# Graph attention on one core: probabilities turned in 32x32 squares on VectorE and moved by DMA instead of turned on TensorE, and the next keys and queries placed between the last slots

## The chip, the core and the metric

One core of a Trainium2 chip runs the whole program. The metric is the device time of one execution in microseconds, lower is better. The engines have their own instruction queues and meet at semaphores: TensorE (PE, matrix products into PSUM), VectorE (DVE), ScalarE (ACT), GpSimd (POOL), and SyncE (SP), which here only issues DMAs.

## The reference

Eight batches of x (1024 x 384, fp32) pass through masked attention with six heads of 64, an output projection, a residual and a layer norm:

```python
q = _heads(seq_inputs @ Wq + bq)
k = _heads(seq_inputs @ Wk + bk)
v = _heads(seq_inputs @ Wv + bv)
scores = jnp.einsum('bhqd,bhkd->bhqk', q, k) / np.sqrt(HEAD_SIZE)
bias = jnp.where(graph_mask, 0.0, NEG)[:, None]
probs = jax.nn.softmax(scores + bias, axis=-1)
ctx = jnp.einsum('bhqk,bhkd->bhqd', probs, v)
...
x = _layernorm(x + (ctx @ Wf + bf), axis=-1)
```

## The kernel before, in words

**Pieces.** Projections and scores are products of fp32r halves: each operand is split into a high part and a low part, and three products (high-high, high-low, low-high) are summed (three_products, L354 to L356). The probabilities times v are plain fp32, which the profile shows as two matmuls for each one written.

**Slots.** A batch is 24 slots. A slot takes 128 queries and the two heads of one pair. Its two units (one head each) go through this chain:

- PE: scores (L444, 12 matmuls) into score_ps, which holds one slot; the next slot's scores wait until both units are masked.
- DVE: one pass adds the mask and takes the row minimum (mask_scores, L660), from PSUM into prob.
- ACT: the exponential with row sums (exponential, L559).
- PE: turn (L457): eight 128x128 transposes of a unit, four into each half of turn_ps.
- ACT and DVE copy the halves into prob_t, keys on the partitions (copy_first L568, copy_odd_second L574, copy_even_second L669).

Two slots (256 queries, one pair) make a pair of slots that is mixed with v: mix (L470), 32 matmuls in two chunks, into context_ps. DVE divides by the row sums (divide, L683). For this the inverse sums must lie along the free axis on every partition: DVE inverts and transposes them (L674, L677), SP writes them to DRAM in four DMAs (L305) and reads them back in two broadcasts (L310). ACT and POOL split the context into high and low (L582, L806).

**Jobs.** Between the slots' chains PE does the jobs of the batch: v (eight), q for the later queries, x transposes of the next batch (L362), output projections p (eight), each with its place in the tables MID, MID_NEXT, AHEAD and TAIL. A k, q or x job is taken out by one ACT pass (high part, L548, L553) and one DVE pass (low part, L645, L650); v by DVE with its bias (L636); p by DVE, which adds the residual and takes moments (L689, L696, L701). The next batch's six k jobs and three first q jobs stand after slot 23, in TAIL. The normalisation is Newton steps and scaling on POOL (L823 to L827, L265). POOL also makes the masks (L788) and adds the output bias to the residual (L802). SP loads x and adjacency and stores the output at fixed slots.

**Order.** The order of each engine is written out by hand in its body(), and an engine works through its queue in order.

## Time and profile before

| | |
|---|---|
| runs | 1510.48 us median of 3 (1510.31 to 1511.2) |
| the profiled execution | 1509.4 us, its span 1507.4 us |
| TensorE busy | 1471.1 us, 98% |
| VectorE busy | 898.2 us, 60% |
| ScalarE busy | 873.4 us, 58% |
| GpSimd busy | 378.2 us, 25% |
| mean granted TensorE clock | 0.997 of full speed |
| the hardware DMA queue | 47,744 packets, 49.12 MB |

All times are of one profiled execution. Busy time is the time in which an engine executes something; matmuls are pipelined, so the price of a group of matmuls is read from the chain of work, where the pieces touch, and not from the duration of one.

### The profile page before, as it was taken

The page shows a single profiled execution, that of the slowest core. Times are in us where ns is not written, and L with a number is a line of the kernel's source. Part 1 is how long each engine was busy: PE and PEld are TensorE (multiplying, and loading weights), DVE is VectorE, ACT ScalarE, POOL GpSimd, SP SyncE. Part 2 cuts the span into 40 slices and gives each one's busy share as a digit, 9 for nine tenths or more (in the row PEclk, how much of TensorE's full clock was granted, in tenths as well). Part 3 has the DMA queues.
Part 4 walks back from the last instruction along what each step waited for, and adds up shares of the span by engine and source line. Part 5 has one row for each costly group of instructions (what it writes and reads, how often), then busy time and mean ns, then how long its engine had stood idle before and what let it go on. Part 6 is the DMA issues. An engine that isn't in the chain of part 4 may idle for free.

```text
span 1507.4 us, 32054 instructions
## 1 busy us (share of the span) xinstructions
PE 1471.1 (98%) x11088; PEld 1141.7 (76%) x11088; DVE 898.2 (60%) x1769; ACT 873.4 (58%) x1637; POOL 378.2 (25%) x676
## 2 busy tenths in 40 slices
PE   7999999999999999999999999999999999999996
PEld 6777787777877778777787777877778777787764
DVE  5666645665556655666555665566655666465654
ACT  4566626666266662666636665366654666546662
POOL 2112242122411224122141221412214122141222
PEclk9999999999999999999999999999999999999998
DMA  3110101100011000100001100011001110000000
GB/s 129 36 40 30 29 27 38 38 29 29 27 50 29 29 29 24 50 30 29 30 24 50 40 29 20 29 49 35 29 19 37 50 29 30 15 25 19 30 22 28
DMA packets 47925, 51.41 MB, mean 34 GB/s; under 512 B 9089, under 2 KB 47745, under 8 KB 47745
## 3 DMA queue, kind: packets, MB, share of 16 engines
q1 hardware_dynamic: 47744, 49.12, 10.5%
q8 instruction: 100, 1.64, 0.5%
q14 instruction: 81, 0.66, 0.1%
HBM read 36.31 MB, written 12.78 MB: 33 GB/s over the span
## 4 chain that ended last, share of the span: by engine, by line
PE 92%; DVE 3%; issue 2%; ACT 1%; POOL 1%; DMA 0%; DVEq 0%; SPq 0%; ACTq 0%; POOLq 0%
PE turn_ps L457 23%; PE context_ps L470 22%; PE score_ps L444 20%; PE misc_ps L356 4%; PE misc_ps L355 4%; PE misc_ps L354 4%; PE score_ps L354 3%; PE score_ps L355 3%; PE score_ps L356 3%; DVE prob L660 1%; PE context_ps L354 1%; PE turn_ps L354 1%; PE context_ps L356 1%; PE context_ps L355 1%; PE misc_ps L362 1%
## 5 line engine op out<-in xcount | busy, mean ns | idle before, releaser
L660 DVE CUSTOM_DVE_ANT_0 prob<-score_ps,mask 128x1024 f32<-128x1024 f32 x384 | 455.0, 1222 | 252.5 <-PE score_ps L444 232.7
L568 ACT ACTIVATE prob_t<-turn_ps 128x512 f32<-128x512 f32 x384 | 229.5, 598 | 431.6 <-PE turn_ps L457 431.6
L559 ACT ACTIVATE prob<-prob,row_min 128x1024 f32<-128x1024 f32 x384 | 442.1, 1151 | 64.3 <-DVE row_min L660 64.3
L457 PE MATMUL turn_ps<-ident,prob 128*128 128x128 f32 x3072 | 413.1, 276 | 9.8 <-ACT prob_t L568 5.5
L457 PEld LDWEIGHTS turn_ps<-ident,prob 128*128 128x128 f32 x3072 | 337.7, 140 | 94.8 <-issue 78.0
L470 PE MATMUL context_ps<-prob_t,v_all 128*64 128x256 f32 x3072 | 372.1, 385 | 0.8 <-ACT prob_t L568 0.8
L470 PEld LDWEIGHTS context_ps<-prob_t,v_all 128*64 128x64 f32 x3072 | 204.6, 136 | 148.9 <-issue 64.0
L806 POOL TENSOR_TENSOR context_lo<-context,context_hi 128x256 fp32r<-128x256 f32 x96 | 70.6, 735 | 938.6 <-ACT context_hi L582 938.6
L669 DVE COPY prob_t<-turn_ps 128x512 f32<-128x512 f32 x192 | 131.7, 686 | 30.7 <-PE turn_ps L457 30.2
L444 PE MATMUL score_ps<-k_hi,q_hi 64*128 64x512 f32 x768 | 140.9, 444 | 4.8 <-issue 3.8
L444 PE MATMUL score_ps<-k_lo,q_hi 64*128 64x512 f32 x768 | 120.4, 390 | 0.0
L444 PE MATMUL score_ps<-k_hi,q_lo 64*128 64x512 f32 x768 | 119.6, 388 | 0.0
L574 ACT ACTIVATE prob_t<-turn_ps 128x512 f32<-128x512 f32 x192 | 115.3, 600 | 0.0
L265 POOL TENSOR_SCALAR res<-res,mean_var,inv_dev 128x384 f32<-128x384 f32 x62 | 102.0, 1651 | 6.7 <-POOL inv_dev L827 6.7
L788 POOL TENSOR_SCALAR mask<-adj_in 128x1024 f32<-128x1024 uint8 x64 | 67.2, 1050 | 86.8 <-DVE row_min L660 62.7
L444 PEld LDWEIGHTS score_ps<-k_hi,q_hi 64*128 64x128 f32 x768 | 57.2, 184 | 38.8 <-issue 37.5
L444 PEld LDWEIGHTS score_ps<-k_lo,q_hi 64*128 64x128 f32 x768 | 72.5, 184 | 17.0
L444 PEld LDWEIGHTS score_ps<-k_hi,q_lo 64*128 64x128 f32 x768 | 72.6, 184 | 16.4
L650 DVE SCALAR_TENSOR_TENSOR k_lo<-score_ps,bias_qk,k_hi 128x512 fp32r<-128x512 f32 x48 | 36.0, 750 | 77.5 <-ACT k_hi L553 77.5
L354 PE MATMUL score_ps<-xt_hi,weight_hi 128*128 128x512 f32 (+1 forms) x216 | 78.6, 364 | 0.7 <-DVE k_lo L650 0.7
L553 ACT ACTIVATE k_hi<-score_ps,bias_qk 128x512 fp32r<-128x512 f32 x48 | 33.1, 690 | 76.3 <-PE score_ps L356 74.6
L355 PE MATMUL score_ps<-xt_lo,weight_hi 128*128 128x512 f32 (+1 forms) x216 | 76.7, 355 | 0.0
(85 smaller groups left out, 1834.9 us busy)
## 6 DMA issues: line engine op xcount, KB each, us to landing
x_in<-in_x_dram SPq DMA_DIRECT2D x32, 384.0 KB, 3.4
inv_rows<-spread_dram SPq DMA_DIRECT2D x192, 64.0 KB, 2.6
out_dram<-res SPq DMA_DIRECT2D x32, 384.0 KB, 2.5
adj_in<-in_adj_dram SPq DMA_DIRECT2D x64, 128.0 KB, 2.2
spread_dram<-inv_turned SPq DMA_DIRECT2D x384, 0.5 KB
prob_t<-in_L_gnn_Wk_dram SPq DMA_DIRECT2D x1, 576.0 KB, 4.3
prob_t<-in_L_gnn_Wq_dram SPq DMA_DIRECT2D x1, 576.0 KB, 7.1
prob_t<-in_L_gnn_Wv_dram SPq DMA_DIRECT2D x1, 576.0 KB, 8.3
```

Source lines behind the costliest of these rows:

```text
L265: engine.tensor_scalar(res[:, n, :], res[:, n, :], mean_var[:, group % 2, tile, 0:1], inv_dev[:, group % 2, tile:tile + 1], ALU.subtract, ...
L354: pe.matmul(dst, left_hi, right_hi, start=(t == 0), stop=False)
L355: pe.matmul(dst, left_hi, right_lo, start=False, stop=False)
L356: last = pe.matmul(dst, left_lo, right_hi, start=False, stop=(t == FT - 1))
L444: last[head] = pe.matmul(score_ps[:, head, keys], q_part[rows, pair, q], k_part[rows, pair, keys], start=(n == 0), stop=(n == 2))
L457: last = pe.transpose(turn_ps[:, half, i, :], prob[:, u % 4, kt * P:(kt + 1) * P], ident[:])
L470: last = pe.matmul(context_ps[64 * head:64 * head + 64, 0:GQ], v_all[:, kt, col:col + HS], prob_t[:, pair % 2, head, kt, :], start=(kt == ...
L559: nc.scalar.activation(prob[:, t % 4, :], prob[:, t % 4, :], ACT.Exp, scale=-1.0, bias=row_min[:, t % 4:t % 4 + 1], accum_out=row_sum[:, t ...
L568: nc.scalar.activation(prob_t[:, pair % 2, head, 0:4, qt * P:(qt + 1) * P], turn_ps[:, 0], ACT.Copy).then_inc(copied[0], 1)
L574: nc.scalar.activation(prob_t[:, pair % 2, head, 4:8, qt * P:(qt + 1) * P], turn_ps[:, 1], ACT.Copy).then_inc(copied[1], 1)
L660: nc.vector.tensor_tensor_reduce(prob[:, t % 4, :], score_ps[:, t % 2, :], mask[:, qt, :], 1.0, HUGE, ALU.add, ALU.min, row_min[:, t % 4:t ...
L669: nc.vector.tensor_copy(prob_t[:, pair % 2, head, 4:8, qt * P:(qt + 1) * P], turn_ps[:, 1]).then_inc(copied[1], 1)
```

## The change

What it does:

- TensorE turns no probabilities. DVE transposes the 32x32 squares of each unit in place (turn_squares, a 128x1024 transpose of 32x32 blocks), and sixteen DMAs a slot move 32-partition blocks of both heads from prob to prob_t: twelve issued by SP, four (a == c) by ACT. Each moves 64 rows of 1 KB. prob becomes a ring of three slots.
- For the keys to match, the tokens are held in another order in xt (tokens: 32-token runs), and mix reads prob_t in runs of 32 columns. A mix is whole (16 products, 32 matmuls in the profile), three slots after its first slot (later for the first two).
- The inverse sums no longer go through DRAM: POOL multiplies the identity by them (make_diagonal) and PE multiplies ones by the diagonals (job "i"), ACT copies the result to context, DVE multiplies.
- v's bias goes into the output bias once at the start (bv_wide). ACT evicts v. For x, k and q ACT makes the high part and a raw copy, and POOL the low part; DVE makes low parts only at the start.
- The jobs go through three banks of PSUM in one order (JOBS), the next batch's k and q in slots 20 to 23, and of the start only k and q of pair 0 remain.
- x is loaded twice, once for the transposes (x_in, half a batch) and once as the residual (res).

The core of the diff. The table of jobs, (kind, number, piece, 1 for the next batch); "i" is spread_inverses, "m" mix, negative numbers belong to the batch before:

```diff
-SLOTS = 24
-EARLY_V = tuple(("v", n, 0) for n in range(4))
-AHEAD = {1: ("v", 4, 0), 2: ("v", 6, 0)}
...
+SLOTS = 24
+RING = 3
+STEADY = {
+    0: [("k", 2, 0, 0), ("k", 2, 1, 0), ("p", -4, 0, 0)],
+    1: [("q", 2, 0, 0), ("i", -1, 0, 0), ("m", -1, 0, 0)],
+    2: [("p", -3, 0, 0), ("v", 0, 0, 0), ("v", 1, 0, 0)],
+    3: [("v", 2, 0, 0), ("v", 3, 0, 0), ("v", 4, 0, 0)],
+    4: [("q", 0, 1, 0), ("v", 5, 0, 0), ("v", 6, 0, 0), ("v", 7, 0, 0)],
+    5: [("i", 0, 0, 0), ("m", 0, 0, 0), ("q", 1, 1, 0)],
+    6: [("i", 1, 0, 0), ("m", 1, 0, 0)],
+    7: [("i", 2, 0, 0), ("m", 2, 0, 0)],
+    8: [("q", 2, 1, 0), ("p", -2, 0, 0), ("p", -1, 0, 0)],
+    9: [("i", 3, 0, 0), ("m", 3, 0, 0)],
+    10: [("x", 0, 0, 1), ("x", 1, 0, 1), ("x", 2, 0, 1), ("q", 0, 2, 0), ("p", 0, 0, 0)],
+    11: [("i", 4, 0, 0), ("m", 4, 0, 0)],
+    12: [("q", 1, 2, 0), ("p", 1, 0, 0)],
+    13: [("i", 5, 0, 0), ("m", 5, 0, 0)],
+    14: [("q", 2, 2, 0)],
+    15: [("i", 6, 0, 0), ("m", 6, 0, 0)],
+    16: [("q", 0, 3, 0), ("p", 2, 0, 0), ("p", 3, 0, 0)],
+    17: [("q", 1, 3, 0), ("i", 7, 0, 0), ("m", 7, 0, 0)],
+    18: [("q", 2, 3, 0), ("x", 0, 1, 1), ("x", 1, 1, 1), ("x", 2, 1, 1)],
+    19: [("i", 8, 0, 0), ("m", 8, 0, 0)],
+    20: [("k", 0, 0, 1), ("k", 0, 1, 1)],
+    21: [("q", 0, 0, 1), ("i", 9, 0, 0), ("m", 9, 0, 0)],
+    22: [("k", 1, 0, 1), ("k", 1, 1, 1)],
+    23: [("q", 1, 0, 1), ("i", 10, 0, 0), ("m", 10, 0, 0)],
+}
```

The squares and their moves, on DVE, SP and ACT:

```diff
+            def turn_squares(b, t):
+                ring = 2 * (t // 2 % RING) + t % 2
+                dve.wait_ge(exp_done, at(b, UNITS, t + 1))
+                dve.sem_inc(dve_waited, 1)
+                nc.vector.transpose(prob[:, ring, :], prob[:, ring, :]).then_inc(squared, 1)
...
+        def move_square(queue, s, a, c):
+            group, qt, ring = s // 2, s % 2, s % RING
+            queue.dma_start(prob_t[32 * c:32 * c + 32, group % 2, :, qt, a, :],
+                            prob[32 * a:32 * a + 32, 2 * ring:2 * ring + 2, GQ * c:GQ * c + GQ]
+                            ).then_inc(landed[ring], 16)
...
+            def move(b, s):
+                sp.wait_ge(squared, at(b, UNITS, 2 * s + 2))
+                if s % 2 == 0:
+                    sp.sem_inc(sp_waited, 1)
+                    sp.wait_ge(mixed, at(b, GROUPS, s // 2 + 1))
+                for a in range(4):
+                    for c in range(4):
+                        if not (a == c):
+                            move_square(sp, s, a, c)
...
+            def body(b):
+                for s in slots_of(b.mode):
+                    work = slot_work(b.mode, s)
+                    if s < SLOTS:
+                        exponential(b, 2 * s)
+                        exponential(b, 2 * s + 1)
+                    for job in work:
+                        if job[0] not in "pm":
+                            evict(b, job)
+                    if s < SLOTS:
+                        move(b, s)
+                    for job in work:
+                        if job[0] == "m":
+                            context_high(b, job[1])
```

The last block is ACT's body; its move waits as SP's does and issues the four with a == c. PE's mix and the spread of the inverses, and DVE's body:

```diff
+            def mix(b, group):
+                pe.wait_ge(context_done, at(b, GROUPS, group + 2))
+                for s in (2 * group, 2 * group + 1):
+                    pe.wait_ge(landed[s % RING], at(b, 256 * SLOTS // RING, 256 * (s // RING + 2)))
...
+                        keys = prob_t[:, group % 2, head, :, :, 32 * kt:32 * kt + 32].rearrange(
+                            "p q a j -> p (q a) j")
...
+            def spread_inverses(b, job):
+                pe.wait_ge(diag_done, at(b, GROUPS, job[1] + 3))
+                for head in range(2):
+                    last = pe.matmul(job_bank(b.mode, job)[64 * head:64 * head + 64, 0:GQ], ones[:],
+                                     diag[:, 2 * head:2 * head + 2, :], start=True, stop=True)
...
+                    if s < SLOTS:
+                        mask_scores(b, 2 * s)
+                        mask_scores(b, 2 * s + 1)
+                        turn_squares(b, 2 * s)
+                        turn_squares(b, 2 * s + 1)
+                    for job in work:
+                        if job[0] == "m":
+                            divide(b, job[1])
+                    if s < SLOTS and s % 2 == 1:
+                        invert_sums(b, s // 2)
+                    for job in work:
+                        if job[0] == "p":
+                            add_residual(b, job)
+                            moments(b, job[1])
```

mask_scores now also waits until the moves of three slots before have landed. Evicting a job on ACT:

```diff
+                    nc.scalar.activation(hi, bank[:, 0:width], ACT.Identity,
+                                         bias=bias_qk[:, which, n:n + 1]).then_inc(hi_done, 1)
+                reg, per, const = in_front(b, len(START_JOBS), SPLITS)
+                act.wait_ge(lo_done, reg * per + (const + at_split - 1))
...
+                    nc.scalar.activation(copy[:, 0:width], bank[:, 0:width], ACT.Identity,
+                                         bias=bias_qk[:, which, n:n + 1]).then_inc(job_out, 1)
```

The first and the last batch are written out apart from the loop of the six between them.

## Rows read from the trace of the kernel before

**Rows 1.** The page, part 1 (busy, share, instructions) and part 4 (chain by line).

```profile
PE 1471.1 (98%) x11088; PEld 1141.7 (76%) x11088; DVE 898.2 (60%) x1769; ACT 873.4 (58%) x1637; POOL 378.2 (25%) x676
...
PE turn_ps L457 23%; PE context_ps L470 22%; PE score_ps L444 20%; PE misc_ps L356 4%; PE misc_ps L355 4%; PE misc_ps L354 4%; PE score_ps L354 3%; PE score_ps L355 3%; PE score_ps L356 3%; DVE prob L660 1%; PE context_ps L354 1%; PE turn_p
```

**Rows 2.** Stretches: length, busy time by engine, granted clock, DMA share, GB/s.

```profile
385.00:570.00 185.00, 183.48 (x1387) 142.40 (x1387) 111.36 (x221) 108.40 (x204) 47.50 (x84) 1.00 0.11 33
...
1480.00:1507.00 27.00, 13.74 (x102) 11.13 (x100) 8.80 (x23) 4.90 (x11) 9.36 (x28) 0.85 0.09 34
```

**Rows 3.** Waits: who waited for whom, us in total, times, longest.

```profile
DVE prob L660 <- PE score_ps L444: 232.7, 185, 2.6
```

**Rows 4.** The chain in order of time: start us, us, what.

```profile
21.24 0.23 PE score_ps L355
...
445.50 0.12 PE misc_ps L356
...
446.49 1.59 PE score_ps L444 x12
448.08 1.88 PE context_ps L470 x16
...
450.98 0.44 PE misc_ps L362 x4
...
463.54 0.18 PE misc_ps L355
```

**Rows 5.** The timeline of one slot: start us, us, instruction.

```profile
443.07 1.22 DVE L660 CUSTOM_DVE_ANT_0 prob<-score_ps,mask 128x1024 f32<-128x1024 f32 x1
...
444.64 1.14 ACT L559 ACTIVATE prob<-prob,row_min 128x1024 f32<-128x1024 f32 x1
...
445.68 0.19 ACT L559 ACTIVATION_READ_ACCUMULATOR prob<-prob,row_min 128x1 f32 x1
...
445.77 0.41 ACT L582 ACTIVATE context_hi<-context 128x256 fp32r<-128x256 f32 x1
446.08 0.46 ACT L553 ACTIVATE q_hi<-misc_ps,bias_qk 128x256 fp32r<-128x256 f32 x1
...
446.57 0.48 DVE L650 SCALAR_TENSOR_TENSOR q_lo<-misc_ps,bias_qk,q_hi 128x256 fp32r<-128x256 f32 x1 [0.80 <-ACT q_hi L553]
```

**Rows 6.** Groups by line and shape: busy us, mean ns of one, idle before.

```profile
L553 ACT ACTIVATE k_hi<-score_ps,bias_qk 128x512 fp32r<-128x512 f32 x48 | 33.1, 690 | 76.3 <-PE score_ps L356 74.6 <-DVE bias_qk L771 1.6
...
L689 DVE TENSOR_TENSOR res<-misc_ps,res 128x384 f32<-128x384 f32 x56 | 31.2, 558 | 43.8 <-PE misc_ps L356 43.0
...
L677 DVE STREAM_TRANSPOSE inv_turned<-inv_sum 128x32 f32<-128x32 f32 x96 | 20.4, 212 | 14.3 <-DVE inv_sum L674 1.7
...
L674 DVE RECIPROCAL inv_sum<-row_sum 128x4 f32<-128x4 f32 x96 | 16.6, 172 | 0.0
...
L701 DVE BATCH_NORM_AGGREGATE mean_var<-stats 128x2 f32<-128x6 f32 x64 | 11.7, 182 | 10.8 <-DVE stats L696 10.8
```

**Rows 7.** DMA issues on SP: two lines' durations, two stretches of its timeline.

```profile
L298 SPq DMA_DIRECT2D adj_in<-in_adj_dram x60: 362/376/895, 67.4 to 1402.8; - x60
...
L310 SPq DMA_DIRECT2D inv_rows<-spread_dram x192: 445/480/1393, 50.9 to 1486.8; - x192
...
438.40 1.27 SPq L305 DMA_DIRECT2D spread_dram<-inv_turned  x4
...
440.55 1.09 SPq L310 DMA_DIRECT2D inv_rows<-spread_dram  x2
```

**Rows 8.** The page, parts 3 (DMA queue) and 6 (us to landing).

```profile
q1 hardware_dynamic: 47744, 49.12, 10.5%
...
inv_rows<-spread_dram SPq DMA_DIRECT2D x192, 64.0 KB, 2.6
```

**Rows 9.** The chain in order of time, first scores and last mix.

```profile
29.30 1.65 PE score_ps L444 x8
...
1487.49 3.69 PE context_ps L470 x32
```

More of the change, by code:

```diff
@@ new lines, in in_front, with through @@
+        def in_front(b, start, table):
+            if b.mode == "first":
+                return 0, 0, start
+            const = start + len(table["first"])
+            if b.mode == "mid":
+                return b.it, len(table["mid"]), const
+            return 0, 0, const + (BATCH - 2) * len(table["mid"])
+        def through(b, start, table, job, back):
+            reg, per, const = in_front(b, start, table)
+            if not back:
+                return reg * per + (const + table[b.mode].index(job) + 1)
+            left = len(table["mid"]) - table["mid"].index(job) - 1
+            assert left == len(table["first"]) - table["first"].index(job) - 1
+            return reg * per + (const - left)
@@ L345, in _ @@
+            body(Batch("first", 0, 0))
+            with sp.Fori(0, len(loop)) as it:
+                body(Batch("mid", it, 1))
+            last = Batch("last", 0, BATCH - 1)
+            body(last)
+            for group in (2, 3):
+                for tile in range(2):
+                    store(last, group, tile)
+            for g in range(4):
+                sp.wait_ge(stored[g], 32 * BATCH)
         @block.tensor
         def _(pe):
-            pe.sem_inc(turned[1], 4)
             pe.sem_inc(mixed, 2)
@@ new lines, in _ @@
+            pe.wait_ge(weights_done, 4)
+            pe.wait_ge(bv_wide_done, 1)
+            for t in range(FT):
+                last = pe.matmul(job_ps[:, 0, 0:H], bv_wide[:, t, :], weight_raw[:, 3, t, :],
+                                 start=(t == 0), stop=(t == FT - 1))
+            last.then_inc(bv_mixed, 1)
+            pe.wait_ge(ones_done, 1)
+            body(Batch("first", 0, 0))
+            with pe.Fori(0, len(loop)) as it:
+                body(Batch("mid", it, 1))
+            body(Batch("last", 0, BATCH - 1))
@@ L612, in _, with start_high @@
-            for kind, what in start_steps():
+            def start_high(job):
+                act.wait_ge(job_done, START_JOBS.index(job) + 1)
+                bank = job_bank("start", job)
+                if job[0] == "x":
+                    half = slice(512 * job[2], 512 * job[2] + 512)
+                    nc.scalar.activation(tokens(xt_hi, job[1], half), as_tokens(bank), ACT.Copy).then_inc(hi_done, 1)
+                else:
+                    width, hi, _ = job_parts(job)
+                    bank = bank[:, 0:width]
+                    which = 1 if job[0] == "k" else 0
+                    nc.scalar.activation(hi, bank, ACT.Identity,
+                                         bias=bias_qk[:, which, job[1]:job[1] + 1]).then_inc(hi_done, 1)
@@ L613, in _ @@
+            for kind, what in START_STEPS:
                 if kind == "weight":
@@ L617, in _ @@
                 else:
[L618 removed]
+                    if what[0] == "k":
                         act.wait_ge(bias_scaled, 2)
[L620 to L623 removed]
+                    start_high(what)
+            body(Batch("first", 0, 0))
+            with act.Fori(0, len(loop)) as it:
+                body(Batch("mid", it, 1))
+            body(Batch("last", 0, BATCH - 1))
         @block.vector
```

871 lines of the change are left out of this document (395 added, 476 removed).

## The prediction

> **What bounds the kernel now.** I read the page's busy times first: TensorE (PE) is busy 98% of the span, VectorE (DVE) 60%, ScalarE (ACT) 58%, and the chain that ended last runs over PE for 92% of the span [rows 1]. The stage table says that this holds in every batch: of 185 us PE is busy 183.5, at granted clock 1.00 (2.4 GHz) [rows 2]. The list of waits says it from the other side: DVE's masking pass waits 232.7 us for scores [rows 3]. So PE's work is the time, and its price is read from the chain, where pieces touch: a slot's scores 1.59 us, half a mix (16 matmuls) 1.88, four x transposes 0.44, one projection matmul 0.12 (q, 256 columns), 0.18 (v or output, 384) or 0.23 (k, 512) [rows 4]. A job of nine is 1.08, 1.57 or 2.07 us.
>
> **Part 1, PE.** The turns leave: 23% of the span [rows 1], 347 us. Each group gets two fp32 matmuls of 256 columns (the spread inverses) in place of the DRAM round trip; mix has 16 such in 3.76 us, so two cost 0.47, times 96 groups is 45 us. Moving the next k and q between slots changes no count. New PE work per batch: 24 scores 38.4, 12 mixes 45.1, 12 spreads 5.6, 8 v and 8 output 25.2, 6 k 12.4, 12 q 13.0, 6 x 2.6, together 142 us against 185 now. PE alone would give 8 x 142 = 1136 plus ends. The moving operands are now read in runs of 32 columns; no row shows such a read, and I take the same price: matmuls stream a column at a time either way. Nothing here says that it could be faster; twice the mix (+45 us a batch) is the other end, which I hold unlikely.
>
> **Part 2, the loop of ACT, DVE and DMA issues.** Now two engines depend on each other in every slot: ACT takes exponentials(s), DVE turns squares(s), ACT issues four of the sixteen moves(s), and only behind these, in its queue, stand exponentials(s+1).
> - Two exponentials: the next ACT instruction starts 1.13 us after one starts, and its sum is out after 1.23 [rows 5]: 1.13 + 1.23 = 2.36, taken as 2.37 with the first one's issue.
> - The second turn of squares. 32 columns take 212 ns, a 4-column operation 172, a 1024-column mask pass 1.22 us [rows 5, 6]. Above: the 40 ns for 28 more columns, as a slope of 1.43 ns, give 0.172 + 1.46 = 1.63 us. Below: the pass itself, 1.22, since nothing in it but its second operand could be saved. I take 1.26, the 1024-column pass plus those 40 ns as a fill, since it has this width. (32 x 212 ns = 6.8 is no bound: 172 of the 212 are paid by 4 columns too.)
> - Four DMA issues on ACT. No row shows one on ACT. On SP one of 128 rows of 1 KB takes 376 ns, one of 64 rows 480 (two in 1.09 us, 0.545 each), four with four short rows each 1.27 us (0.32 each) [rows 7]. A square has 64 rows of 1 KB; I take 0.41 from start to start (376 and a gap), so 1.64 us; ends 0.32 and 0.545.
> - Three hand-overs at 0.05 us (q_hi ends at 446.54, q_lo starts at 446.57 [rows 5]): 0.15.
>
> Sum 5.42 us a slot; where a group is mixed, context_high adds 0.41 [rows 5]: 5.83. DVE's mask passes (2.4 for two) hide: the first lies beside ACT's issues. The copies that leave DVE and ACT (L568, L574, L669) and the low parts and v biases that leave DVE cost nothing and gain nothing: DVE waited anyway. What they make room for is 384 x 1.26 = 484 us of turning.
>
> **Part 3, jobs in slots.** An output job puts an addition of 0.56, statistics over the same 384 columns (charged the same), an aggregation of 0.18 with as long a wait, and for every second one two more small operations on DVE, 1.65 us [rows 6]; one in a slot makes it 5.42 + 1.2 = 6.6, two 8.25. Each x, k, q job now has two ACT passes before the moves (0.69 for k's 512 columns, 0.46 for q's 256 [rows 5, 6]; x, without a bias, taken as 0.6), hidden only for the 1.3 us in which DVE turns. Slot by slot, the larger of PE and the loop, in us:
> 0: 7.17 (PE: k, k, p), 1: 6.91, 2: 6.6 (DVE), 3: 6.31, 4: 7.39, 5: 6.91 (PE); 6, 7, 9, 11, 13, 15, 19: 5.83 each (both); 8, 16: 8.25 (DVE, two output jobs); 10: 9.1 (ACT: three x and a q are 4.5 us of passes, and the fourth job waits for a bank); 18: 8.5 (same without the bank); 12: 6.6; 14: 5.4; 20, 22: 6.8 (ACT, two k); 17, 21, 23: 5.9 (PE's 6.91 less 1.0 that it is ahead).
> Sum 159.5; 1.5 us for other waits on the three job banks and on landings: **161 us a batch**, against 185.
>
> **Part 4, queues and landings.** SP issues 12 moves and on average 1.33 other DMAs a slot: 12 x 0.41 + 0.55 = 5.5 us, under 6.7. Its DMAs move behind the moves: stores and loads of x, residual and adjacency are wanted slots later. A slot's moves land 4.9 us of issue and 2.6 of landing [rows 8] behind the second turn, 7.5 us; the mix two slots on wants them after some 5 to 10, so this cover is thin and the 1.5 us stand for it; the mask pass three slots on wants them after 13. DMA engines: 1,024 packets of 1 KB a slot, 64 on each of 16. The queue took 10.5% of 16 x 1507.4 us for 47,744 packets, 53 ns each [rows 8]: 3.4 us a slot and the 11% of today. ACT waits for a free half of prob_t in slot 4 only (group 0 is mixed in slot 5), where PE is the bound. POOL's new work (low parts, diagonals) brings it from 47.5 of 185 us [rows 2] to some 95 of 161: hidden.
>
> **Sum.** 8 x 161 = 1288. Start: first scores now at 29.3 us [rows 9], behind 15 jobs; with nine, 24. The last batch lacks the next one's x, k and q: -12. End: today the last mix starts 20 us before the end [rows 9]; behind the last slot stand a landing, a mix, two output jobs and two normalisations, 30 us. 1288 + 24 - 12 + 30 = 1330, plus 2.0 around the span (1509.4 beside 1507.4); the median shown is 1.1 over that profiled execution: **1333 us**, 12% less.
>
> **Rivals.**
> 1. *The two queues' issues exclude each other* (the slower side). SP and ACT start their moves on the same semaphore, so ACT's four would take eight turns, 3.3 us in place of 1.64. The 15 slots that the loop bounds get 1.64 more, others 0.45 to 1.3: 28.7 a batch, 1333 + 8 x 28.7 = **1562**. It decides from 1510 - 1333 = 177 us, 22 a batch, which is 1.26 us more on ACT a slot: four issues in 2.9 us, 0.72 each. A single issue on SP reached 1.39 us [rows 7], which speaks for it; that most take 0.38 to 0.48 while nothing competes says neither. 15%.
> The Trainium skill (Perfetto Trace Analysis, DMA Instruction — HWDGE) has this rule: the descriptor generator is shared by the issuing sequencers, and each locks it for exclusive use within the profiled issue. By it the sum would be rival 1's; no run here yet has two issuing engines.
> 2. *An issue costs 0.545* as the 64-row ones do, without exclusion: SP needs 12 x 0.545 + 0.6 = 7.1 us a slot, 171 a batch, the new bound; with uneven slots 173: 1333 + 96 = **1429**. 13%.
> 3. *Turning takes 1.63*: the first turn then ends 0.5 later than the second exponential, the second takes 0.37 more, 0.87 in some 15 slots: 108 us, **1441**. 10%.
> 4. *DMA engines bind*: from 94 ns a packet. A square reads 32 partitions and writes 32 with all engines, which no row shows. At twice 53 ns a slot needs 6.8 + 0.7 = 7.5, 180 a batch: **1485**. 6%.
> 5. That PE's gain is not real because its clock falls: it was 0.85 where PE was busy half of the time [rows 2]; here it stays 88% busy. 1%.
>
> **Numbers.** Forecast 55%. About 0.2% is what a measurement of this kernel can tell from no change. Low end: issues at 0.32 and no bank waits leave 156 a batch, 1293; if slots even out through PE's lead, 3 us less: 1268. High end: takes in rivals 2 to 4 with their roundings, 1495; outside stay rival 1's 15% and a few below. Faster: 55 + 13 + 10 + 4 of rival 4's 6 and 1 of rival 1's lower half, 83%; within 0.2%: 2%; slower 15%.
>
> **What the new profile should show.** PE near 86% busy at clock 1.00; DVE near 67% with a transpose group of 384 at 1.26 us; ACT near 50% with 768 issues of about 0.4; SP's moves 0.41 from start to start; slots 8, 10, 16, 18 longest. Rival 1: ACT's issues of 0.7 or more, and the exponentials waiting behind them. Rival 2: SP's issues end-to-end without a gap. Rival 4: landings of far over 2.6 us, and mix or mask passes released by DMA. I am wrong if DVE's mask pass still waits mostly for scores with PE over 95% busy, or if a batch is over 185 us.

## The result: slower by a fifth, with SyncE's DMA queue as the new bound

The changed kernel takes 1814.03 us (median of 4 runs, 1811.84 to 1816.15) against 1510.76 us of the kernel before on the same chip (4 runs, 1510.31 to 1511.2). The ratio is 1.2007, with a 95% interval of 1.1986 to 1.2028. The forecast was 1333 us with a range of 1268 to 1495: wrong in sign, and far outside the range. The profiled execution has a span of 1814.0 us.

The page of the changed kernel, parts 1, 2 (the granted clock), 3 (DMA queues), 4 (the chain that ended last) and 6 (DMA issues, with the median time to landing), answers to [rows 1] and [rows 8]:

```profile
PE 1345.2 (74%) x8406; PEld 951.3 (52%) x8406; DVE 1059.9 (58%) x1617; ACT 722.3 (40%) x1404; POOL 655.0 (36%) x958
...
PEclk9897998878988889888898878978789788898977
...
q1 hardware_dynamic: 223488, 199.07, 43.1%
q10 hardware_dynamic: 61440, 50.38, 11.4%
...
SPq 76%; issue 10%; PE 5%; DVE 2%; ACTq 2%; ACT 2%; DMA 1%; POOL 1%; POOLq 0%; DVEq 0%
SPq L293 70%; PE context_ps L510 2%; ACTq L293 2%; DVE prob L688 2%; SPq L362 1%; SPq L329 1%; SPq L355 1%; PE score_ps L494 1%; DMA prob_t<-prob 1%; ACT prob L602 1%; SPq L349 1%; PE job_ps L399 0%; DMA x_in<-in_x_dram 0%; PE job_ps L401 0
...
prob_t<-prob SPq DMA_DIRECT2D x2304, 64.0 KB, 2.0
prob_t<-prob ACTq DMA_DIRECT2D x768, 64.0 KB, 2.1
```

The part to read is part 4. Before, PE held 92% of the chain. Now no engine that computes holds more than 5%: 76% is SyncE's queue, and 70% is one line, L293, the move of a square. Part 1 alone would have said "TensorE is still the busiest", and that 74% is partly the lower clock (0.86 over the span, where it was 1.00).

The stretch of 225 us answers to the first row of [rows 2]; it is about one batch:

```profile
700.00:925.00 225.00, 168.32 (x1054) 118.05 (x1054) 131.36 (x201) 90.24 (x177) 84.74 (x122) 0.86 0.56 139
```

Every engine has free time in it, and the 16 DMA engines are busy 56% of it. Line L293 alone, with the durations of its issues (min/median/max ns) and the start of the first and the last, answers to the first rows of [rows 7]:

```profile
L293 SPq DMA_DIRECT2D prob_t<-prob x2304: 585/597/1980, 32.3 to 1788.7; - x192
L293 ACTq DMA_DIRECT2D prob_t<-prob x768: 592/619/2363, 33.5 to 1780.7; - x192
```

A stretch of SyncE's timeline (start us, us, instruction, how many in a row) answers to the others:

```profile
821.96 7.66 SPq L293 DMA_DIRECT2D prob_t<-prob  x12
829.90 0.35 SPq L349 DMA_DIRECT2D x_in<-in_x_dram  x1
830.51 0.34 SPq L355 DMA_DIRECT2D res<-in_x_dram  x1
830.96 8.39 SPq L293 DMA_DIRECT2D prob_t<-prob  x12
839.63 0.36 SPq L362 DMA_DIRECT2D out_dram<-res  x1
840.25 0.34 SPq L355 DMA_DIRECT2D res<-in_x_dram  x1
840.84 7.64 SPq L293 DMA_DIRECT2D prob_t<-prob  x12
```

A move occupies the queue for 0.597 us; 11 starts and one duration make 7.66, so it is 0.642 us from start to start. The blocks of twelve follow one another with only the other DMAs between them. The one exception comes once a batch, before its first block:

```profile
913.40 0.45 SPq L355 DMA_DIRECT2D res<-in_x_dram  x1
917.05 7.95 SPq L293 DMA_DIRECT2D prob_t<-prob  x12
```

These are 3.2 us without an issue (3.2 to 3.7 in the other batches); the squares of the new batch's first slot are turned only at 916.3. In the stretch of 225 us stand 24 blocks with 196.4 us together, 8.18 each: 7.66 where all issues are of the median kind, and 0.5 for single issues of 0.8 to 2 us among them. The other DMAs, 1.33 a slot, and the instructions around them take what is left, 225/24 - 8.18 = 1.2 us (0.1 of it is that gap). So a slot is 7.7 + 0.5 + 1.2 = 9.4 us on SyncE. The prediction had 5.5.

The list of waits (us in total, times, longest) shows who stands behind the queue:

```profile
ACT prob L602 <- DVE row_min L680: 462.8, 157, 8.3
...
DVE context L698 <- PE context_ps L510: 317.6, 80, 14.0
PE context_ps L510 <- DMA prob_t<-prob: 306.4, 75, 7.6
DVE prob L680 <- PE score_ps L494: 162.8, 119, 5.6
```

The page's groups (busy us, mean ns of one, idle before) show the price of the new operations:

```profile
L510 PE MATMUL context_ps<-prob_t,v_all 128*64 128x256 f32 x3072 | 490.8, 489 | 306.5 <-DMA prob_t<-prob 306.4
L602 ACT ACTIVATE prob<-prob,row_min 128x1024 f32<-128x1024 f32 x384 | 439.6, 1146 | 530.5 <-DVE row_min L680 462.8
...
L688 DVE STREAM_TRANSPOSE prob<-prob 128x1024 f32<-128x1024 f32 x384 | 457.9, 1231 | 151.4 <-ACT prob L602 151.4
```

The mix now waits 306 us for landings, although a move lands 2.0 us after its issue, sooner than the 2.6 of [rows 8]. The wait is for moves that have not been issued yet. DVE's wait for scores ([rows 3]) fell from 232.7 to 162.8 us.

### The profile page after: what moved, and what is told of

It is laid out like the page before. It is cut to its first block, busy times and chain, and to the rows that moved or that the text cites. A ratio compares the mean times of both kernels' runs of the same rounds, so it can differ in the third digit from the quotient of the medians.

```text
span 1814.0 us, 29642 instructions
## 1 busy us (share of the span) xinstructions
PE 1345.2 (74%) x8406; PEld 951.3 (52%) x8406; DVE 1059.9 (58%) x1617; ACT 722.3 (40%) x1404; POOL 655.0 (36%) x958
## 3 DMA queue, kind: packets, MB, share of 16 engines
q1 hardware_dynamic: 223488, 199.07, 43.1%
q10 hardware_dynamic: 61440, 50.38, 11.4%
## 4 chain that ended last, share of the span: by engine, by line
SPq 76%; issue 10%; PE 5%; DVE 2%; ACTq 2%; ACT 2%; DMA 1%; POOL 1%; POOLq 0%; DVEq 0%
SPq L293 70%; PE context_ps L510 2%; ACTq L293 2%; DVE prob L688 2%; SPq L362 1%; SPq L329 1%; SPq L355 1%; PE score_ps L494 1%; DMA prob_t<-prob 1%; ACT prob L602 1%; SPq L349 1%; PE job_ps L399 0%; DMA x_in<-in_x_dram 0%; PE job_ps L401 0%; PE job_ps L400 0%
## 5 line engine op out<-in xcount | busy, mean ns | idle before, releaser
L510 PE MATMUL context_ps<-prob_t,v_all 128*64 128x256 f32 x3072 | 490.8, 489 | 306.5 <-DMA prob_t<-prob 306.4
L680 DVE CUSTOM_DVE_ANT_0 prob<-score_ps,mask 128x1024 f32<-128x1024 f32 x384 | 454.2, 1220 | 214.0 <-PE score_ps L494 162.8
L510 PEld LDWEIGHTS context_ps<-prob_t,v_all 128*64 128x64 f32 x3072 | 301.3, 180 | 496.2 <-issue 386.7
L688 DVE STREAM_TRANSPOSE prob<-prob 128x1024 f32<-128x1024 f32 x384 | 457.9, 1231 | 151.4 <-ACT prob L602 151.4
L809 POOL TENSOR_TENSOR diag<-ident,inv_sum 128x512 f32<-128x512 f32 x96 | 99.9, 1040 | 488.4 <-DVE inv_sum L693 487.0
L803 POOL TENSOR_TENSOR q_lo<-raw,q_hi 128x256 fp32r<-128x256 f32 x95 | 69.3, 730 | 360.0 <-ACT raw L594 360.0
L399 PE MATMUL job_ps<-xt_hi,weight_hi 128*128 128x256 f32 (+1 forms) x423 | 149.4, 353 | 24.6 <-ACT raw L592 24.0
L401 PE MATMUL job_ps<-xt_hi,weight_lo 128*128 128x256 f32 (+1 forms) x423 | 137.1, 324 | 0.0
L400 PE MATMUL job_ps<-xt_lo,weight_hi 128*128 128x256 f32 (+1 forms) x423 | 137.0, 324 | 0.0
L399 PEld LDWEIGHTS job_ps<-xt_hi,weight_hi 128*128 128x128 f32 x423 | 80.9, 191 | 71.6 <-issue 36.7
L401 PEld LDWEIGHTS job_ps<-xt_hi,weight_lo 128*128 128x128 f32 x423 | 81.3, 192 | 6.7
```

Source lines behind the costliest of these rows:

```text
L399: pe.matmul(dst, left_hi, right_hi, start=(t == 0), stop=False)
L400: pe.matmul(dst, left_hi, right_lo, start=False, stop=False)
L401: last = pe.matmul(dst, left_lo, right_hi, start=False, stop=(t == FT - 1))
L510: last = pe.matmul(context_ps[64 * head:64 * head + 64, 0:GQ], v_all[:, kt, col:col + HS], keys, start=(kt == 0), stop=(kt == TT - 1))
L680: nc.vector.tensor_tensor_reduce(prob[:, ring, :], score_ps[:, head, :], mask[:, s % 2, :], 1.0, HUGE, ALU.add, ALU.min, row_min[:, ring:r ...
L688: nc.vector.transpose(prob[:, ring, :], prob[:, ring, :]).then_inc(squared, 1)
```

## The experiments

The theory after the result: the price of an on-chip move (both ends in the on-chip memory) on its issuing queue, times twelve, makes SyncE the bound. Rivals: the two issuing queues exclude each other; the DMA engines or their packets bind; the mix or the turn is slower than forecast. Where no range is given, a time is that of one execution, beside 1510 to 1511 us of the kernel before. Where moves are left out "from the second batch on", the first batch keeps all of them and still takes 206 to 210 us, which is in the time.

**Fewer issues on SyncE.** From the second batch on, four of its twelve moves are left out, and the semaphore is advanced for them:

```diff
-                        if not (a == c):
+                        if not (a == c) and (b.mode == "first" or c != (a + 1) % 4):
                             move_square(sp, s, a, c)
+                if b.mode != "first":
+                    sp.sem_inc(landed[s % RING], 64)
```

> From the second batch on, four of SP's twelve moves a slot are left out (the squares with c one after a), so stale probabilities stay in their place; everything else is as in the changed kernel. Theory (SP's issue time is the bound: a move costs SP 0.642 us from start to start, twelve of them and the other DMAs fill the 9.4 us slot): a slot loses 4 x 0.642 = 2.6 us on SP and falls to some 6.7 us, where the loop of ScalarE and VectorE takes over (with four issues of 0.65 us some 178 us a batch): 1440 to 1500 us. Rival A (the DMA engines' throughput is the bound): the bytes moved fall by a quarter of the moves' share, to about 1400 to 1450 us, and leaving out ScalarE's four instead must give the same. Rival B (TensorE at its lower clock is the bound): less than 3% off, since no TensorE work goes.

Measured: 1568.1 us, 246 less than the changed kernel, by leaving out a quarter of the moves. The chain of this kernel by engine:

```profile
issue 22%; DVE 18%; ACTq 17%; PE 15%; SPq 13%; ACT 9%; POOL 5%; DVEq 1%; DMA 1%; POOLq 0%
```

SyncE is down from 76% to 13%. But 1440 to 1500 was expected. Under the bound that was taken away lies a second one, at some 187 us a batch where 178 were expected; the first batch, with all its moves, adds 19 us more.

**No issues on ScalarE.** The same for ACT's four moves, all twelve of SyncE stay:

```diff
+                if b.mode != "first":
+                    act.sem_inc(landed[s % RING], 64)
+                    return
```

> From the second batch on, ScalarE's four moves a slot (the squares with a equal to c) are left out instead, as many bytes and packets as in the run before; SP keeps twelve. Theory (SP's issue time): no change beyond 2%, 1780 to 1820 us, SP's moves still 0.64 us from start to start. Rival A (DMA engines' throughput): as the run before, 1400 to 1450 us. Rival C (the two queues' issues exclude each other): SP's pitch falls as ScalarE issues nothing, by a third of its price, to about 1450 to 1550 us. Rival D (the four issues in ScalarE's queue hold up the exponentials, as rival 1 of the prediction had it): 1500 us or less.

Measured: 1798.44 us, 1% less. Line L293 of this kernel, SyncE's issues with no second queue beside them, and behind it the page's chain by engine:

```profile
L293 SPq DMA_DIRECT2D prob_t<-prob x2304: 585/597/2115, 32.3 to 1770.9; - x192
```

```profile
SPq 84%; issue 10%; PE 2%; ACT 1%; DVE 1%; DMA 1%; POOL 1%; ACTq 1%; POOLq 0%; DVEq 0%
```

The minimum and the median are 585/597, as with ACT's issues, and there are still long ones (up to 2115). A median hides how many: by the trace's records, of SyncE's 2304 issues 71 take over 0.75 us here and 120 in the changed kernel, and the mean falls from 631 to 620 ns. This is 25 us of issue in all, beside the 16 us by which the time fell. So ACT's queue costs SyncE's something, but 2% of an issue and not a third. The run also removes a quarter of all moved bytes, for those 16 us. Neither exclusion nor the DMA engines set the time.

**Half the bytes.** Each move carries rows of 512 bytes instead of 1 KB from the second batch on (half of each square's columns is not moved):

```diff
-                            prob[32 * a:32 * a + 32, 2 * ring:2 * ring + 2, GQ * c:GQ * c + GQ]
+                            prob[32 * a:32 * a + 32, 2 * ring:2 * ring + 2, GQ * c:GQ * c + width]
```

> From the second batch on, every move carries half of its columns (rows of 512 B in place of 1 KB, the other half of the probabilities stays stale); sixteen moves a slot and 64 rows in each as before. Theory (SP's issue time, paid per DMA and per row, not per byte): 1790 to 1820 us, an issue still 0.60 us. Rival A (DMA engines' throughput): the packets take half or two thirds of their 65 ns, 1250 to 1450 us. Rival E (landings come late for the mix): 3 to 8% faster.

Measured: 1815.69 us, no change. The page's row of the queue, and line L293's issues:

```profile
q1 hardware_dynamic: 223488, 133.01, 28.0%
```

```profile
L293 SPq DMA_DIRECT2D prob_t<-prob x2304: 585/597/2110, 32.2 to 1787.5; - x192
```

The queue's share of the engines fell from 43.1% to 28.0%, the issue kept its 597 ns, the time stood still.

**Two moves handed to ScalarE.** The full computation, with ten moves on SyncE and six on ACT:

```diff
+        def on_act(a, c):
+            return a == c or (a, c) in ((0, 1), (2, 3))
```

> The whole computation, with ten moves a slot on SP and six on ScalarE. Theory (SP's issue time): SP's slot falls by 2 x 0.642 to about 8.0 us, while ScalarE's loop grows to 2.37 + 1.2 + 0.15 + 6 x 0.65 = 7.6 us and more in the slots with jobs: 1600 to 1720 us. Rival A (DMA engines' throughput): no change, 1814 us. Rival D (ScalarE's issues hold up the exponentials and are the bound already): slower than 1814 us, by some 1.3 us a slot, 2050 us.

Measured: 1755.16 us. The page's chain by engine, and the first of the list of waits:

```profile
ACTq 34%; issue 21%; DVE 19%; ACT 11%; PE 10%; POOL 2%; SPq 1%; DVEq 1%; DMA 0%; POOLq 0%
```

```profile
DVE prob L691 <- ACT prob L605: 519.3, 192, 7.2
```

3% come back, less than was expected (1600 to 1720), and the bound is at once on the other queue. ACT's six issues (3.8 to 5.7 us from the first to the end of the last, half of the blocks under 4.0) stand between one slot's exponentials and the next slot's, and DVE's turn waits 519 us for exponentials. SyncE binds at twelve and four, ACT at ten and six. Eleven and five was not run; with the same prices it would still have 11 x 0.642 + 0.5 + 1.2 = 8.8 us a slot on SyncE, an estimate.

**Half of all moves.** Six on SyncE, two on ACT; half of each slot's squares are not moved from the second batch on. This shows what the rest of the kernel takes when issues bind far less:

```diff
-                        if not (a == c):
+                        if not (a == c) and (b.mode == "first" or (c - a) % 4 == 1 or (a, c) in ((0, 2), (2, 0))):
...
-                        if a == c:
+                        if a == c and (b.mode == "first" or a < 2):
```

> From the second batch on, half of the moves are left out: six of SP's twelve and two of ScalarE's four a slot, so stale probabilities stay in their place. SP's slot is then 6 x 0.642 and 1.7 us of the rest, 5.5 us, and ScalarE's two issues of 0.65 us cost 1.3 us, less than the 1.64 us that the prediction charged for four. If only the price of an issue was wrong in the prediction: 1280 to 1350 us, with TensorE near 88% busy. If the loop of ScalarE, VectorE and TensorE has waits that the prediction lacked, or the lower granted clock costs by itself: 1400 to 1500 us.

Measured: 1471.39 us, 174.5 us a batch where 161 were forecast, with PE 84% busy at clock 0.93. If only the price of an issue had been wrong, 1280 to 1350 was expected; so something else was wrong too. The page's chain by engine:

```profile
PE 34%; issue 20%; DVE 14%; SPq 10%; ACT 7%; POOL 7%; ACTq 5%; DVEq 1%; DMA 1%; POOLq 0%
```

From mask pass to mask pass its fifth batch has, for slots 0 to 23: 7.3 6.8 7.0 6.0 8.1 9.7 10.5 5.6 8.6 5.4 12.5 5.7 7.4 5.4 5.2 6.9 8.4 5.4 8.6 5.9 6.1 6.8 6.0 9.4. Against the table of Part 3 twenty of the 24 are within 1.1 us; slots 5, 6, 10 and 23 are 2.8 to 4.7 us over it. The timeline around slots 4 and 5 shows how the first of them come about:

```profile
617.51 0.65 PE L432 MATMUL job_ps<-diag,ones 128*64 128x256 f32 x4
...
617.99 3.62 PE L512 MATMUL context_ps<-prob_t,v_all 128*64 128x256 f32 x32
...
621.66 1.52 ACTq L293 DMA_DIRECT2D prob_t<-prob  x2
...
623.37 1.15 ACT L604 ACTIVATE prob<-prob,row_min 128x1024 f32<-128x1024 f32 x1 [6.85 <-issue]
...
624.75 2.38 DVE L692 STREAM_TRANSPOSE prob<-prob 128x1024 f32<-128x1024 f32 x2 [4.58 <-ACT prob L604]
```

The moves of slot 4 need the half of prob_t that the first group's mix frees. That mix stands in slot 5, behind slot 5's scores, and ends at 621.6. ACT's two moves start at 621.66, and the exponentials of slot 5, whose mask passes were through at 619.0 and 620.2, stand behind them in ACT's queue until 623.37, at the end of 6.85 us in which ACT computes nothing; the last 4.3 of these lie behind the first mask pass.

**That wait by itself.** The last kernel with the first group's spread and mix moved from slot 5 to slot 4, the second's from 6 to 5, and q's projection back to slot 6:

```diff
-    4: [("q", 0, 1, 0), ("v", 5, 0, 0), ("v", 6, 0, 0), ("v", 7, 0, 0)],
-    5: [("i", 0, 0, 0), ("m", 0, 0, 0), ("q", 1, 1, 0)],
-    6: [("i", 1, 0, 0), ("m", 1, 0, 0)],
+    4: [("q", 0, 1, 0), ("v", 5, 0, 0), ("v", 6, 0, 0), ("v", 7, 0, 0), ("i", 0, 0, 0), ("m", 0, 0, 0)],
+    5: [("i", 1, 0, 0), ("m", 1, 0, 0)],
+    6: [("q", 1, 1, 0)],
```

> The run with half of the moves left out (1471 us), with one more edit: the first group's inverses and mix stand at the end of slot 4, the second's in slot 5, and the q job of slot 5 in slot 6. The prediction had said that ScalarE waits for a free half of the turned buffer in slot 4 only and that TensorE is the bound there. In that run slots 5 and 6 took 9.7 and 10.5 us in place of the forecast 6.9 and 5.8, with exponentials 6.9 us idle behind the moves that wait for the first mix. If that wait is the cause: slots 5 and 6 fall by 5 to 8 us together and the time to 1415 to 1440 us. If they are long for the jobs' sake: 1465 to 1475 us.

Measured: 1443.1 us, just outside the expected stretch, 28 less. In the fifth batch slots 4 to 6 take 12.3, 5.8 and 5.0 us (23.1) instead of 8.1, 9.7 and 10.5 (28.3); batches 2 to 6 take 170.3 us in the mean instead of 174.8. So this wait is real, and some 4.5 of the 13.5 us by which a batch exceeded the forecast.

**What an issue is paid for: rows.** One head per move, 32 rows of 1 KB instead of 64 (the second head's squares are not moved):

```diff
-                            prob[32 * a:32 * a + 32, 2 * ring:2 * ring + 2, GQ * c:GQ * c + GQ]
+                            prob[32 * a:32 * a + 32, 2 * ring:2 * ring + heads, GQ * c:GQ * c + GQ]
```

> From the second batch on, every move carries one head only (32 rows of 1 KB in place of 64; the other head's probabilities stay stale); sixteen moves a slot. If an issue is paid by its rows or by the second stride: SP's median issue falls from 0.597 to 0.30 to 0.40 us and the time to 1330 to 1450 us. If an issue is paid per DMA alone: 0.597 us still and 1800 to 1820 us.

Measured: 1784.21 us. Then the same number of rows with all the bytes: the full computation, with the two heads' columns interleaved so that a square is 32 rows of 2 KB.

```diff
-            queue.dma_start(prob_t[32 * c:32 * c + 32, group % 2, :, qt, a, :],
-                            prob[32 * a:32 * a + 32, 2 * ring:2 * ring + 2, GQ * c:GQ * c + GQ]
+            src = prob[32 * a:32 * a + 32, 2 * ring + c // 2, (c % 2) * 2 * GQ:(c % 2) * 2 * GQ + 2 * GQ]
+            queue.dma_start(prob_t[32 * c:32 * c + 32, group % 2, qt, a, :, :].rearrange("p h k -> p (h k)"), src
```

> The whole computation. The buffer of probabilities is laid out so that the two heads' 256 columns of a square lie side by side (and so in the turned buffer): a move has 32 rows of 2 KB in place of 64 of 1 KB, the same bytes; masking, exponential and turning read and write four pieces of 256 columns in place of one of 1024. If an issue is paid by its rows or its second stride: 0.30 to 0.40 us an issue and 1330 to 1450 us, faster than both kernels. If it is paid per DMA alone: 1800 to 1820 us. If it is paid by bytes: 0.60 us too.

Measured: 1784.47 us (1781.3 to 1785.37), ratio to before 1.1808 (1.1789 to 1.1828), 1.6% below the changed kernel. SyncE's issues of the kernel with one head a move, and then of the one with rows of 2 KB:

```profile
L293 SPq DMA_DIRECT2D prob_t<-prob x2304: 507/591/2175, 31.7 to 1756.1; - x192
```

```profile
L301 SPq DMA_DIRECT2D prob_t<-prob x2304: 507/591/2288, 31.3 to 1756.9; - x192
```

Half the rows save 6 of 597 ns in the median, with half the bytes or with all of them: an issue is paid by the piece. In the mean they save 12 and 14 of 631 ns, over 2304 issues 28 and 32 us; this is the 30 us by which both times lie under the changed kernel's (1800 to 1820 was expected).

**What an issue is paid for: its ends.** Thirty-two extra DMAs at the very end, four of each kind, when nothing else runs (its 1843.0 us are none to compare). The first and the last two kinds' edit:

```diff
+            for n in range(4):
+                sp.dma_start(prob_t[32:64, n % 2, :, n // 2, 0, :], prob[0:32, 0:2, 0:GQ]).then_inc(shaped, 16)
...
+                sp.dma_start(shape_dram[n, 0:32, :], prob[0:32, 0, 0:2 * GQ]).then_inc(shaped, 16)
...
+                sp.dma_start(prob_t[32:64, n % 2, 0, n // 2, 0:2, :], shape_dram[n, 0:32, :].rearrange("p (a k) -> p a k", a=2)).then_inc(shaped, 16)
```

> The changed kernel with 32 more DMAs on SP after its last store, when nothing else runs: four each of 32, 128, 64, 16, 4 and 8 partitions within the on-chip memory (two rows of 1 KB each), 32 partitions to DRAM and 32 from DRAM (2 KB rows). This prices an issue by itself: if other engines or ScalarE's queue stretched it, the 32-partition one falls below 0.5 us here; if the price is that of the shape, it is 0.60 us again. If fewer than 128 partitions are what costs, 128 take 0.34 us as the loads do; if both ends on chip are what costs, 128 take 0.60 us and the DRAM ones 0.35 us.

The issues' durations: on chip with 32, 128 and 4 partitions, then to DRAM and from DRAM with 32, and last on chip with 8:

```profile
L393 SPq DMA_DIRECT2D prob_t<-prob x4: 592/596/605, 1808.9 to 1810.9; - x4
...
L396 SPq DMA_DIRECT2D prob_t<-prob x4: 626/630/687, 1812.9 to 1815.0; - x4
...
L405 SPq DMA_DIRECT2D prob_t<-prob x4: 637/645/704, 1826.1 to 1828.2; - x4
...
L408 SPq DMA_DIRECT2D shape_dram<-prob x4: 344/423/432, 1830.1 to 1831.4; - x4
...
L411 SPq DMA_DIRECT2D prob_t<-shape_dram x4: 302/422/422, 1833.2 to 1834.4; - x4
...
L414 SPq DMA_DIRECT2D prob_t<-prob x4: 685/694/713, 1836.3 to 1838.5; - x4
```

Without any load an on-chip move of 32 partitions costs 596 ns, as in the loop (597). With 4, 16, 64 or 128 partitions it is 609 to 645, with 8 it is 694. With one end in DRAM it is 422 to 423, where 0.35 had been expected. The DRAM pair has 32 rows of 2 KB; a move of that shape on chip costs 591 ns (the run before this one). What separates 0.4 from 0.6 us is where the two ends are.

**Half as many moves, all of the work.** The full computation; a move carries a square of both slots of a group, 128 rows of 1 KB. The ring of probabilities has four places instead of three, paid for with a mask in bytes and one raw buffer:

```diff
-            queue.dma_start(prob_t[32 * c:32 * c + 32, group % 2, :, qt, a, :],
-                            prob[32 * a:32 * a + 32, 2 * ring:2 * ring + 2, GQ * c:GQ * c + GQ]
-                            ).then_inc(landed[ring], 16)
+            queue.dma_start(prob_t[32 * c:32 * c + 32, g % 2, :, a, :],
+                            prob[32 * a:32 * a + 32, 4 * (g % 2):4 * (g % 2) + 4, GQ * c:GQ * c + GQ]
+                            ).then_inc(landed[g % 2], 16)
```

> The whole computation with half as many moves: the ring of probabilities holds four slots and the squares of two slots (one group) go in one DMA of 128 rows of 1 KB, so sixteen DMAs in every second slot, the same bytes. To make room in the memory the mask is kept in bytes (0 or 255 in place of 9e15; exp of less than -240 is 0 in fp32 all the same) and the raw copy has one buffer in place of two. If an issue is paid per DMA (0.60 us, as 32 and 64 rows showed): SP needs 11 us in two slots and is no bound, and the time is near that of the kernel with half of the moves left out, 1440 to 1540 us; the burst behind every second slot costs what lies above 1471. If the DMA engines or the landings count after all, since all bytes move now: 1600 us or more.

Measured: 1589.3 us (1587.45 to 1592.95), ratio 1.0521 (1.0502 to 1.0539), between the two expectations. It is 12% faster than the changed kernel and 5% slower than the one before, and the fastest complete version of the change that was tried. Line L292, its moves, and one group of them in the timeline; the page's chain by engine; and from the list of waits PE's for landings:

```profile
L292 SPq DMA_DIRECT2D prob_t<-prob x1152: 585/610/1897, 39.4 to 1560.8; - x192
L292 ACTq DMA_DIRECT2D prob_t<-prob x384: 592/740/1667, 42.6 to 1554.6; - x192
...
820.63 3.33 ACTq L292 DMA_DIRECT2D prob_t<-prob  x4
820.75 8.84 SPq L292 DMA_DIRECT2D prob_t<-prob  x12
```

```profile
PE 24%; issue 23%; SPq 14%; DVE 14%; POOL 8%; DMA 6%; ACT 6%; ACTq 5%; DVEq 1%; POOLq 0%
```

```profile
PE context_ps L509 <- DMA prob_t<-prob: 159.0, 59, 8.0
```

Twice the rows cost 13 ns more in the median, but the mean of SyncE's issues rises from 631 to 727 ns. The trace's records show where: issues that overlap one of ACT's have a mean of 838 ns, the others 669, and ACT's own 829. With moves of 128 rows issues on two queues at once are dearer, which with 64 rows they hardly were (636 against 628). Whether they do so where issues are made or through the load on the DMA engines stays open. No queue holds most of the chain now (SyncE's 14%, ACT's 5%), but the moves of a group all come at its end, and the mix still waits 159 us for landings.

**Two tries to improve on it.** First the earlier mixes, with the table edit shown above:

> The full computation: as e7_group (one move per square and pair of slots, 12 on SP and 4 on ACT), with the first group's spread and mix moved from slot 5 to slot 4, the second's from slot 6 to 5, and one projection of q back to slot 6, as in e10_early_mix. If ACT's moves waiting for the mix that frees their half of prob_t hold the exponentials here too, it gives back what it gave in e10_early_mix, 3.5 to 5 us a batch: 1550 to 1562. If in e7_group the first mixes wait for their landings anyway, the time stays at 1585 to 1595.

Measured: 1623.45 us (1621.77 to 1624.66), ratio 1.0747 (1.0729 to 1.0764): 2% slower, where a gain or nothing was expected. Slot 4, with three v jobs and now a mix, takes 15.4 us instead of 11.4, slot 7 takes 12 instead of 6; a batch is 196.5 us instead of 192.7. Then, on top of this, all sixteen moves of a group on SyncE and none on ACT:

```diff
-                        if not (a == c):
-                            move_square(sp, s // 2, a, c)
+                        move_square(sp, s // 2, a, c)
```

> The full computation: as e11_group_early, with ACT's four moves of a pair of slots issued by SP too, sixteen on SP. SP then needs 16 x 0.642 = 10.3 us and some 3 to 3.5 for its other DMAs a pair of slots, 13.3 to 13.8 us, which is 160 to 166 us a batch and below today's 185. If ACT's issues (2.4 us in every second slot, between a turn and the next exponentials) are what holds the batch, it is faster than e11_group_early by up to 12 x 1.2 = 14 us a batch: 1440 to 1500. If the slots that hold SP are uneven (the moves of a group are issued in a block of 10.3 us that the mixes wait for), the landings come 2.6 us later for each group and the time stays within 20 us of e11_group_early or is above it.

Measured: 1628.35 us (1624.47 to 1633.0), ratio 1.0782 (1.0755 to 1.0809), within 20 us of the kernel before it, as the last of the three expectations had it. Line L292, its moves, and from the list of waits PE's for landings:

```profile
L292 SPq DMA_DIRECT2D prob_t<-prob x1536: 585/604/2115, 38.8 to 1601.1; - x192
```

```profile
PE context_ps L508 <- DMA prob_t<-prob: 213.2, 62, 7.4
```

What ACT is spared (blocks of four issues, 3.4 us each in the mean, in every second slot) is given back in landings: a block of sixteen issues takes 10.3 to 12.9 us, where SyncE's twelve took 9.2 in the mean, and the mix waits 213 us for landings instead of 171. Alone, SyncE's issues have a mean of 640 ns for the same 128 rows, and 57 of 1536 take over 0.75 us, where beside ACT's it was 359 of 1152. Issuing moves from GpSimd was not tried, so whether a third queue would carry them stays open. So does a complete version that beats the kernel before: none was found.

## Why the prediction was wrong

**The step that failed is the price of a DMA issue, in Part 2 and above all in Part 4.** "12 x 0.41 + 0.55 = 5.5 us, under 6.7" was to show that SyncE has room. It measured 12 x 0.642 = 7.7, 0.5 for long issues and 1.2 for the rest, 9.4 us. Of the 3.9 us that were missing, 2.8 are the price of the twelve, 0.5 the long issues and 0.6 the other DMAs with the instructions around them. The 0.41 came from the loads of 128 rows in [rows 7]: they were chosen because their rows have 1 KB, as a square's have. The runs with half the bytes and half the rows and the extra DMAs at the end show that neither rows nor bytes are the price, but both ends on chip, and of such a DMA [rows 7] had none; the nearest, of 64 rows with one end in DRAM, had 0.545. The text said that no row shows the case on ACT; it should have said so for SyncE, twelve times a slot, as well. The slack of 1.2 us in 6.7 was gone at 0.51 an issue.

**What the step is worth.** A batch takes 224 us with all moves, 174.5 with half of them, and 161 were forecast. So of 63 us a batch some 50 are the moves' issues and 13.5 everything else. The totals say it less well: 1814 - 1471 = 343 of the 481 us between forecast and result, because the first batch of the halved kernel keeps all its moves and takes 206 us. The 13.5 are a lower end for the rest, as that kernel spares ACT two issues a slot as well, and SyncE's and ACT's queues still hold 15% of its chain.

**Rival 2 had the mechanism.** "SP's issues end-to-end without a gap" is what the timeline shows. It was given 13% and 1429 us with 0.545; with 0.642, the long issues and the dearer other DMAs it gives 24 x 9.4 = 225 a batch, 1333 + 8 x (225 - 161) = 1845 against the 1814 measured (the first batch takes 207 us, and the last has less to issue). The upper bound was 0.1 us too low, and twelve a slot make of that 1.2 us.

**Rivals 1, 3 and 4 fell.** ACT's issues have a median of 0.619 and a mean of 0.643 us, not 0.7 or more, and SyncE's have the same median with and without them. The Trainium skill (Perfetto Trace Analysis, DMA Instruction — HWDGE) has the sequencers share a generator that is locked for exclusive use. What rival 1 made of it, ACT's four issues taking eight turns, the trace does not bear out: a block of four takes 2.66 us in the mean, where eight turns at the measured 0.642 would be 5.1 (an estimate), and SyncE's mean issue falls by 11 ns without them. With moves of 128 rows the two queues did stretch each other's issues (838 ns where they overlap, 669 elsewhere), and the trace does not tell whether this lock is the cause. Turning took 1.231 us, not 1.63. The DMA engines were 56% busy, a packet of 1 KB took 65 ns in the mean where rival 4 needed 94, and half the bytes changed nothing.

The Trainium skill (DMA: Bandwidth & Descriptors, "Issuing engines are not separate DMA queues") says that spreading DMAs over engines saves only the sequencer's time, "usually small relative to the DMA itself". One move is not far from it: 0.6 us of issue beside 2.0 to landing. Twelve in a queue do not: 8.2 us of issue a slot beside the same 2.0, and the issue is the bound.

**Part 1 was right in its counts and prices,** but for slips of 0.2 us (24 scores at 1.59 are 38.2, not 38.4, and the pieces of slot 0 give 7.3, not 7.17). Spread and mix together took 4.10 us in the timeline (617.51 to 621.61), for 0.47 + 3.76 = 4.23 forecast. The mix with its keys read in runs of 32 columns took 3.62 us for 32 matmuls at full clock, where two halves of [rows 4] are 3.76: the read in runs cost nothing here. What was not foreseen is that PE's work becomes dearer as it waits: at the granted clock of 0.86 a mix's matmul has a mean of 489 ns, with half the moves (0.93) 408, in the kernel before (0.997) 385. Rival 5 was given 1% on the ground that PE would be 88% busy, which hung on the step that failed. While SyncE binds and PE holds 5% of the chain, the clock can cost little. In the kernel with half of the moves PE holds 34% of the chain, and how much of the 13.5 us is the clock's was not measured.

**Part 2 was right in its turn** (1.231 us for 1.26) **and in the exponentials** (1.146), wrong in four issues on ACT (2.66 us in the mean, at least 2.53, instead of 1.64). **Part 3** held for most slots once the issues were halved. Part of its excess comes from Part 4's sentence that ACT waits for a free half of prob_t "in slot 4 only (group 0 is mixed in slot 5), where PE is the bound": the wait is there, but the exponentials of the next slot stand behind it, and the experiment that moved the mix gave 28 us back. The excess in slots 10 and 23, and with it the rest of the 13.5 us a batch, was not taken apart.

**The relief itself was real and worth nothing here.** PE lost its turns, and its batch was 142 us of work by count; but a saving on one engine counts only down to the next bound, and this change built that bound. That the relief can show is seen in the kernels with half of the moves, 1471 and 1443 us against 1511, but they do not compute the whole result.

## What to carry to other kernels

A queue that issues DMAs is an engine: count its issues per stage, multiply by the start-to-start time of a DMA *between the same two kinds of memory*, add the other DMAs, and hold it against the stage's time before anything else. A row with the right size but another end is no such price, and if it is missing, the range must hold half as much again (0.642 came for 0.41 here). Fewer and larger moves are the cure (half the issues of twice the rows: 1814 to 1589 us), a second queue only if what stands behind the issues on that engine can wait. And look at the mean of an issue beside its median: in the kernel with the larger moves the median was 610 ns and the mean 727.

## What the runs showed of the hardware that was not expected

- An on-chip move holds SyncE's queue 0.60 us (0.642 start to start). One with an end in DRAM holds it 0.42 with 32 partitions where nothing else runs and 0.35 for the loads of 128 in the loop; in the kernel before the medians on [rows 7] are 0.38 and 0.48. Between 4 and 128 partitions, 32 and 128 rows, and 512 bytes and 2 KB a row the on-chip median on SyncE stays within 0.59 to 0.70.
- Among issues of 0.6 us stand some of 0.8 to 2.1 us, some 0.5 us a slot in all. They are there with ACT's issues left out (3% of SyncE's issues over 0.75 us instead of 5%), with half the bytes and with half the rows. None is among the 32 extra DMAs at the end, where one or two would be expected at 5%, too few to tell. Their cause stays open.
- DVE turns 128x1024 fp32 values in squares in 1.231 us, as long as its mask pass over them (1.220).
- Two queues that issue on-chip moves at once slow each other little with 64 rows (SyncE's mean 0.636 us where issues overlap, 0.628 elsewhere) and more with 128 rows (0.838 and 0.669). ACT's issues, nearly all of which overlap SyncE's, have a median of 0.619 and 0.740 us. The first of ACT's block of four is its cheapest (0.60); with 128 rows the last takes 1.27 in the mean.
